# A sorted mixture-of-experts stage in a two-layer decoder: row contents, order of the start, way back of the results and home of w1

## The reference

```python
xr = x @ wg_red.T                                   # x: layer norm of the stream, 2048 x 128
wg_unit = wg / jnp.maximum(jnp.linalg.norm(wg, axis=1, keepdims=True), EPS)
logits = xr @ wg_unit.T                             # 2048 x 8
gates = jax.nn.softmax(logits, axis=1)
indices_s = jnp.argmax(gates, axis=1)
scores = jnp.max(gates, axis=1)
for e in range(E):
    mask = (indices_s == e).astype(x.dtype)[:, None]
    h = jax.nn.gelu(x @ w1[e] + b1[e], approximate=False)   # w1[e]: 128 x 512
    out = out + mask * (h @ w2[e] + b2[e])                  # w2[e]: 512 x 128
out = out * scores[:, None]
```

## Time and profile before

| | us |
|---|---|
| median of 3 runs | 1184.0 (1183.9 to 1187.14) |
| the profiled execution | 1186.93 |
| its span, first to last instruction | 1185.2 |
| busy: PE / VectorE / ScalarE / POOL | 962.1 / 793.7 / 626.2 / 355.7 |
| the last part (norm to stream addition) | from 1023 to 1178 |

### The profile page before, as it was taken

How to read it: one execution, slowest core, us unless ns; L and a number is a source line. 1 busy time by engine, 2 the same in 40 slices (tenths; PEclk the granted TensorE clock), 3 DMA queues, 4 the chain that set the end, 5 groups by cost and what they waited for, 6 DMA issues and landing times. The chain is left out here.

```text
span 1185.2 us, 20933 instructions
## 1 busy us (share of the span) xinstructions
PE 962.1 (81%) x6175; PEld 495.7 (42%) x6175; DVE 793.7 (67%) x1693; ACT 626.2 (53%) x1548; POOL 355.7 (30%) x533
## 2 busy tenths in 40 slices
PE   4489999999999736899799999999999677352870
PEld 2122233333333134566545555555555435331760
DVE  8789999999999286566556665666656689243111
ACT  4548888888888702222365656656566233110540
POOL 4212222222222131000244454545545423225004
PEclk9759999999999956799899999999999889766995
DMA  1000000000000000000100000000000100105762
GB/s 45 1 1 1 1 2 2 0 0 0 0 0 0 1 15 14 6 16 20 35 14 8 12 10 7 13 7 13 7 8 1 32 0 1 54 1 155 204 188 71
DMA packets 47723, 28.63 MB, mean 24 GB/s; under 512 B 12152, under 2 KB 44208, under 8 KB 47664
## 3 DMA queue, kind: packets, MB, share of 16 engines
q1 hardware_dynamic: 46640, 25.81, 7.9%
q0 software_dynamic: 1024, 2.10, 0.6%
HBM read 22.79 MB, written 5.11 MB: 24 GB/s over the span
## 5 line engine op out<-in xcount | busy, mean ns | idle before, releaser
L509 DVE TENSOR_REDUCE a_nmax<-a_rows 128x2 f32<-128x1024 f32 x256 | 299.2, 1218 | 14.6 <-PE a_rows L415 11.4
L552 ACT ACTIVATE a_probs<-a_turned 128x512 f32<-128x512 f32 x512 | 269.2, 603 | 40.7 <-PE a_turned L437 39.1
L1116 POOL TENSOR_TENSOR a_prob<-a_prob,a_rinv 128x256 f32<-128x256 f32 (+3 forms) x128 | 159.7, 1253 | 173.1 <-DVE a_rinv L1306 172.8
L1299 DVE TENSOR_REDUCE a_nmax<-a_score 128x2 f32<-128x256 f32 (+3 forms) x128 | 105.6, 825 | 124.2 <-PE a_score L1155 119.8
L1253 ACT ACTIVATE a_prob<-a_score,a_nmax 128x128 f32<-128x128 f32 (+3 forms) x256 | 132.7, 523 | 82.4 <-DVE a_nmax L1299 82.0
L437 PE MATMUL a_turned<-a_q,a_qk 32*128 32x512 bf16 x512 | 137.4, 391 | 7.6 <-ACT a_probs L552 5.6
L400 PE MATMUL a_acc<-a_probs,a_vg 128*32 128x512 f32 x1024 | 139.0, 615 | 0.8 <-ACT a_probs L552 0.7
L415 PE MATMUL a_rows<-a_qk 32*128 32x512 bf16 x512 | 111.9, 401 | 13.2 <-DVE a_nmax L509 6.2
L1152 PE MATMUL a_score<-a_k_s,a_q_s 64*128 64x384 f32 (+3 forms) x512 | 103.7, 481 | 2.2 <-ACT a_prob L1253 1.3
L437 PEld LDWEIGHTS a_turned<-a_q,a_qk 32*128 32x128 bf16 x512 | 35.3, 91 | 155.1 <-ACT a_probs L552 131.8
L1312 DVE COPY a_pt<-a_turn 128x128 f32<-128x128 f32 (+3 forms) x224 | 92.2, 447 | 1.4 <-PE a_turn L1166 1.4
(11 more groups left out here) (288 smaller groups left out, 1518.9 us busy)
## 6 DMA issues: line engine op xcount, KB each, us to landing
m_w<-L_ffn_w SPq DMA_DIRECT2D x46, 256.0 KB, 3.6
a_wq<-L_attn_Wq SPq DMA_DIRECT2D x16, 128.0 KB, 2.2
xs_sorted<-m_zeros SPq DMA_DIRECT2D x1, 1472.0 KB, 6.6
m_xs<-xs_sorted SPq DMA_DIRECT2D x5, 256.0 KB, 3.6
ys_sorted<-m_ysb SPq DMA_DIRECT2D x5, 256.0 KB, 3.3
g_X<-x SPq DMA_DIRECT2D x4, 256.0 KB, 3.6
m_wgu<-L_ffn_gate_up_proj SPq DMA_DIRECT2D x8, 128.0 KB, 2.1
a_wk<-L_attn_Wk SPq DMA_DIRECT2D x32, 32.0 KB, 2.0
```

What stands on the lines that cost most here:

```text
L509: dve.tensor_reduce(nmax[i % 2][:, p // 2, (p % 2) * 2:(p % 2) * 2 + 2], rows[n % 2][:, :, :], AX_X, ALU.max, negate=True).then_inc(row_ou ...
L552: act.activation(probs[:, (tb % 2) * 4 + j, :], turned[n % 3][:, :], ACT.Exp, scale=float(HD0) ** -0.5).then_inc(turn_out, 1)
L1116: pool.tensor_tensor(pr, pr, spread(rinv[:, t % RING, :], 2, width), ALU.mult).then_inc(scl, 1)
L1299: dve.tensor_reduce(nmax[:, t % RING, :], score[t % 2][:, :, 0:width], AX_X, ALU.max, negate=True).then_inc(mx, 1)
```

## The change

- The rows that are scattered carry 130 numbers instead of 128 (`ROW1`, 520 bytes): the norm, the token's number and its score. The norm is written straight into them (`xe`). Unused slots hold a number of their own beyond 2047, in `blank`.
- Results are scattered to token order by POOL in the tile loop, one indirect DMA a tile, into `y_tokens`. The address is the token number out of the sorted row. VectorE multiplies y by the score as it copies it, into a ring of four buffers, guarded by `y_out`. At the end SP loads y in token order in four DMAs, and four wide additions follow.
- The small loads go first on SP, and the blank rows follow; the statistics and the norm stand ahead of the gate weights' work on VectorE, PE, ScalarE and POOL, except for one reduction over `wg` behind `in_s`, which stands between VectorE's statistics and its normalising. The two gate matrices are folded into one of 128 x 8 (`wge`), and the logits come from XT directly.
- w1 of all experts (2 MB) is loaded once. VectorE copies the expert's 128 x 512 into one of three buffers for each tile, at an address that it loads into a register from `eid_i`. SP loads only w2 for each tile, and the up-projection waits for the copy (`s_w1`), the down-projection for w2.
- VectorE copies x of tile t after w1 of tile t, and y of tile t - 2 behind them.

Declarations and semaphore names are left out below.

```diff
 
...
             for n in range(SB * b, SB * b + SB):
-                dve.tensor_scalar(self.g.XN[:, n, :], self.g.X[:, n, :], self.mv[:, n, 0:1],
+                dve.tensor_scalar(self.rows[:, n, 0:D], self.g.X[:, n, :], self.mv[:, n, 0:1],
                                   self.rstd[:, n:n + 1], ALU.subtract, ALU.mult).then_inc(self.norm, 1)
 
     def tensor(self, pe):
...
             pe.wait_ge(self.norm, SB * (b + 1))
             wait(pe, self.xt, b - 1)
...
-        ln = LayerNorm(sc, g, ln_ps)
+        xe = sc.sb("xe", [P, NT, ROW1])
+        ln = LayerNorm(sc, g, ln_ps, rows=xe)
...
-        w1 = [sc.sb(f"w1{i}", [P, FH]) for i in range(WB)]
+        w1_all = sc.sb("w1_all", [P, E, FH])
+        w1 = [sc.sb(f"w1{i}", [P, FH]) for i in range(3)]
...
-        xs = sc.sb("xs", [P, TILES1, D])
+        xs = sc.sb("xs", [P, TILES1, ROW1])
+        token = sc.sb("token", [P, TILES1], I32)
...
-        ysb = sc.sb("ysb", [P, TILES1, D])
+        ysb = sc.sb("ysb", [P, 4, D])
...
-        xs_d = nc.dram_tensor("xs_sorted", (SLOTS1, D), F32).ap()
-        ys_d = nc.dram_tensor("ys_sorted", (SLOTS1, D), F32).ap()
+        xs_d = nc.dram_tensor("xs_sorted", (SLOTS1, ROW1), F32).ap()
+        y_d = nc.dram_tensor("y_tokens", (NT * P + SLOTS1, D), F32).ap()
...
-            sp.wait_ge(zs, 1)
-            sp.dma_start(xs_d.rearrange("(t p) d -> p t d", p=P), zeros[:, :, :]).then_inc(zd, 16)
...
+            sp.wait_ge(blank_s, 2)
+            sp.dma_start(xs_d.rearrange("(t p) d -> p t d", p=P), blank[:, :, :]).then_inc(blank_d, 16)
+            for e in range(0, E, 2):
+                sp.dma_start(w1_all[:, e:e + 2, :], g.dram["L1_ffn_w1"][e:e + 2].rearrange("e d h -> d e h")
+                             ).then_inc(w1_in, 16)
...
-                sp.dma_start(w1[t % WB][:, :], g.dram["L1_ffn_w1"][bass.ds(e, 1)].rearrange("o d h -> (o d) h")
-                             ).then_inc(w_in[t % WB], 16)
                 sp.dma_start(w2[t % WB][:, :, :],
                              g.dram["L1_ffn_w2"][bass.ds(e, 1)].rearrange("o (f p) d -> p (o f) d", p=P)
                              ).then_inc(w_in[t % WB], 16)
...
-            for t in range(T):
-                if t + WB < T:
-                    load_weights(t + WB)
-                for t0, t1 in GROUPS:
-                    if t + 1 == t1:
-                        sp.wait_ge(s_y, t1)
-                        sp.dma_start(ys_d[t0 * P:t1 * P, :].rearrange("(t p) d -> p t d", p=P), ysb[:, t0:t1, :]
-                                     ).then_inc(ys_out, 16)
+            for t in range(WB, T):
+                load_weights(t)
+
+            for i in range(4):
+                sp.wait_ge(y_out[i], 16 * len(range(i, T, 4)))
+            for b in range(B):
+                sp.dma_start(yg[:, SB * b:SB * b + SB, :],
+                             y_d[S * b:S * (b + 1), :].rearrange("(t p) d -> p t d", p=P)).then_inc(back[b], 16)
...
-            pool.memset(zeros[:, :, :], 0.0).then_inc(zs, 1)
+            pool.memset(blank[:, :, :], 0.0).then_inc(blank_s, 1)
             pool.memset(hmask[:, :], 1.0).then_inc(hm, 1)
+            pool.wait_ge(blank_s, 1)
+            pool.iota(blank[:, :, D], pattern=[[P, T]], base=NT * P, channel_multiplier=1,
+                      allow_small_or_imprecise_dtypes=True).then_inc(blank_s, 1)
...
+            pool.iota(xe[:, :, D], pattern=[[P, NT]], base=0, channel_multiplier=1,
+                      allow_small_or_imprecise_dtypes=True).then_inc(s_ext, 1)
+            ln.gpsimd(pool)
+            pool.wait_ge(wnd, 2)
+            pool.tensor_tensor(wnorm[:, 2:3], wnorm[:, 0:1], wnorm[:, 1:2], ALU.pow).then_inc(wn, 1)
...
-            pool.wait_ge(wnd, 2)
-            pool.tensor_tensor(wnorm[:, 2:3], wnorm[:, 0:1], wnorm[:, 1:2], ALU.pow).then_inc(wn, 1)
-            ln.gpsimd(pool)
-
-            pool.wait_ge(zd, 16)
+            pool.wait_ge(blank_d, 16)
+            pool.wait_ge(s_ext, 2)
             pool.wait_ge(s_pos, 1)
             for n in range(NT):
                 pool.indirect_dma_start(out=xs_d, out_offset=bass.IndirectOffsetOnAxis(ap=pos_i[:, n:n + 1], axis=0),
-                                        in_=g.XN[:, n, :], in_offset=None).then_inc(scat, 16)
-            pool.wait_ge(ys_out, 16 * len(GROUPS))
-            for n in range(NT):
-                pool.indirect_dma_start(out=yg[:, n, :], out_offset=None, in_=ys_d,
-                                        in_offset=bass.IndirectOffsetOnAxis(ap=pos_i[:, n:n + 1], axis=0)
-                                        ).then_inc(back[n // SB], 16)
+                                        in_=xe[:, n, :], in_offset=None).then_inc(scat, 16)
+            for t in range(T):
+                pool.wait_ge(s_id, t // 4 + 1)
+                pool.wait_ge(s_y, t + 1)
+                pool.indirect_dma_start(out=y_d, out_offset=bass.IndirectOffsetOnAxis(ap=token[:, t:t + 1], axis=0),
+                                        in_=ysb[:, t % 4, :], in_offset=None).then_inc(y_out[t % 4], 16)
...
+            ln.tensor(pe)
             pe.wait_ge(in_s, 16 * (3 + NT))
-            pe.transpose(flat[0][:, 0:GD], wgr[:, :], g.ident[0:GD, 0:GD]).then_inc(prep, 1)
-            pe.transpose(flat[1][:, 0:E * FC], b1r[:, :], g.ident[0:E * FC, 0:E * FC]).then_inc(prep, 1)
+            pe.transpose(up[0][:, 0, 0:E * FC], b1r[:, :], g.ident[0:E * FC, 0:E * FC]).then_inc(prep, 1)
             pe.wait_ge(wnd, 5)
-            pe.transpose(flat[2][0:GD, 0:E], wgu[:, :], g.ident[0:E, 0:E]).then_inc(prep, 1)
-            ln.tensor(pe)
+            pe.transpose(up[1][0:GD, 0, 0:E], wgu[:, :], g.ident[0:E, 0:E]).then_inc(prep, 1)
+            pe.wait_ge(prep_c, 2)
+            pe.matmul(xps[0][:, 0:E], wgr[:, :], wgut[:, :], start=True, stop=True).then_inc(prep, 1)
             pe.wait_ge(prep_c, 3)
             for b in range(B):
                 ln.ready(pe, b)
-                pe.matmul(flat[b][0:GD, :], wgrt[:, :], g.XT[:, b * S:(b + 1) * S], start=True, stop=True
-                          ).then_inc(s_xr, 1)
-            pe.wait_ge(s_xrc, B)
-            for n in range(NT):
-                last = pe.matmul(ln_ps[0][:, n * E:(n + 1) * E], xr[:, n * P:(n + 1) * P], wgut[:, :],
-                                 start=True, stop=True)
+                for n in range(SB * b, SB * b + SB):
+                    last = pe.matmul(xps[1][:, n * E:(n + 1) * E], g.XT[:, n * P:(n + 1) * P], wge[:, :],
+                                     start=True, stop=True)
...
-                pe.transpose(xps[t % 2][:, 0:P], xs[:, t, :], g.ident[:, :]).then_inc(s_xp, 1)
+                pe.transpose(xps[t % 2][:, 0:P], xs[:, t, 0:D], g.ident[:, :]).then_inc(s_xp, 1)
...
-                pe.wait_ge(w_in[t % WB], 32 * (t // WB + 1))
+                pe.wait_ge(s_w1, t + 1)
...
             def down_of(t):
+                pe.wait_ge(w_in[t % WB], 16 * (t // WB + 1))
...
-            for i, (dst, src) in enumerate(((wgrt[:, :], flat[0][:, 0:GD]), (b1t[:, :, :].rearrange("p e f -> p (e f)"), flat[1][:, 0:E * FC]),
-                                            (wgut[:, :], flat[2][0:GD, 0:E]))):
+            ln.scalar(act)
+            for i, (dst, src) in enumerate(((b1t[:, :, :].rearrange("p e f -> p (e f)"), up[0][:, 0, 0:E * FC]),
+                                            (wgut[:, :], up[1][0:GD, 0, 0:E]), (wge[:, :], xps[0][:, 0:E]))):
                 act.wait_ge(prep, i + 1)
                 act.activation(dst, src, ACT.Copy).then_inc(prep_c, 1)
-            ln.scalar(act)
-            for b in range(B):
-                act.wait_ge(s_xr, b + 1)
-                act.activation(xr[:, b * S:(b + 1) * S], flat[b][0:GD, :], ACT.Copy).then_inc(s_xrc, 1)
...
+            ln.vector_stats(dve)
             dve.wait_ge(in_s, 16 * (3 + NT))
             dve.tensor_tensor_reduce(out=wsq[:, :], in0=wg[:, :], in1=wg[:, :], scale=1.0, scalar=0.0,
                                      op0=ALU.mult, op1=ALU.add, accum_out=wnorm[:, 0:1]).then_inc(wnd, 1)
+            ln.vector_norm(dve)
...
-            ln.vector_stats(dve)
-            ln.vector_norm(dve)
-            rt.top1(dve, ln_ps[0][:, 0:NT * E].rearrange("p (n e) -> p n e", e=E))
+            rt.top1(dve, xps[1][:, 0:NT * E].rearrange("p (n e) -> p n e", e=E))
...
+            dve.wait_ge(s_ext, 1)
+            dve.tensor_copy(xe[:, :, D + 1], rt.score[:, :]).then_inc(s_ext, 1)
...
+            def copy_w1(t):
+                if t == 0:
+                    dve.wait_ge(w1_in, 16 * E // 2)
+                wait(dve, s_up, t - 2)
+                e = dve.value_load(eid_i[0:1, t:t + 1], min_val=0, max_val=E - 1)
+                dve.tensor_copy(w1[t % 3][:, :], w1_all[:, bass.ds(e, 1), :].rearrange("p o h -> p (o h)")
+                                ).then_inc(s_w1, 1)
...
             def copy_y(t):
                 dve.wait_ge(s_dn, t + 1)
-                dve.tensor_copy(ysb[:, t, :], down[t % 2][:, 0:D]).then_inc(s_y, 1)
-
-            copy_x(0)
+                if t >= 4:
```

(44 more changed lines are left out.)

16 lines of the change are left out of this document (9 added, 7 removed).

## The result

The changed kernel takes 1145.7 us (median of 4, 1144.86 to 1147.15) against 1183.95, a ratio of 0.9686 with a 95% interval of 0.9642 to 0.9729. Its profiled execution took 1146.02 us with a span of 1144.3; the one of before took 1186.93. So 40.9 us went between the two profiles, where 41.8 was forecast.

The account below looks back on a forecast made before the run. One chain bounds the last stage: loads behind zeros, a loop bound by weight traffic, then gathers. -15.0 + 0.6 - 11.9 - 15.5 = -41.8 takes 1186.9 to 1145.1 us profiled, 1142.2 median; range 1137 to 1159.

Parts of the forecast that it names:

- Head: Last stage's start up to the logits: small loads first and norm ahead of gate work save 15.0 us (bounds -10.9, -16.3).
- the term of the logits: End of the head: 32 logit passes, now with 128-row weights, keep about 5.5 us.
- Routing and scatter: Between logits and tile loop: w1 copies beside scatters add 0.4 us, a cast 0.2; +0.6 (bounds 0, +5).
- The cover of the score's copy: Routing: copying the score into the rows hides in VectorE's wait for the rank matmuls, costing nothing; uncovered 0.2 us.
- Rival B: Scatter and sorted-row load: 520-byte rows may move as two pieces, doubling landing and first load; +5 us, 1147; chance 0.08.
- Loop: Tile loop: without w1 on the DMA queue, 19 steps take 1.92 us each; -11.9 us (bounds -13.5, -10).
- VectorE's 1.9 us in line: Tile loop: y copy 0.29, register load 0.73, w1 copy 0.39, x copy 0.28 and gaps, one after another per tile.
- rival E: Tile loop: w2 alone still arrives late, landing over 5.5 us after issue, so no loop gain; 1154 us; chance 0.03.
- the sum for w2: Tile loop: w2's register load to issue 0.73, 0.38, landing at most 4.3; 5.4 us against some 6.6 available.
- Rival A: Tile loop: VectorE bounds it, each w1 copy waiting for a scatter (0.96); adds 9 or 18 us, 1151 to 1160; chance 0.19.
- the rule: Tile loop: VectorE's two-port copies lock out GpSimd's DMA descriptor writes, so w1's copies would delay POOL's scatters.
- Tail: After the last y copy: one scatter, four loads and one addition take 9.8 us against 25.3; -15.5 (bounds -16.5, -12.4).

Follow-up runs that it names:

- h1: Changed kernel, but SP waits for the blank rows and writes them before the small loads, as before; 1153.65 us, head 28.70 against 22.07.
- u1: Changed kernel, but w1 is loaded by DMA for each tile again, without the VectorE copies; 1153.58 us, loop 53.88 against 43.61.
- u2: Changed kernel, but y is stored in sorted order and gathered by POOL at the end again; 1160.86 us, tail 24.31 against 9.69.
- l2: Changed kernel with the register load on VectorE done twice for each tile; 1148.18 us, loop 47.07 against 43.61.
- n1: Changed kernel with the 16 b2 loads on their own semaphore, so the normalising no longer waits for them; 1148.74 us, head 19.84 against 22.07.
- l1: Changed kernel with w1 copied twice for each tile, register load once; 1146.27 us, loop 44.70 against 43.61.
- l4: Changed kernel with w1 copied four times for each tile; 1154.71 us, loop 51.99 against 43.61.
- l3: Changed kernel meant to copy w1 four times; by a slip one extra copy, behind a wait standing three times; 1150.11 us, loop 45.51 against 43.61.

## Why the prediction was right, point by point

*What bounded the kernel.* All three stretches were named rightly, and undoing each change alone gives its time back: 6.6 us of the head with h1 (8.0 at equal logits), 10.3 of the loop with u1, 14.6 of the tail with u2. The rest of the head's gain, from the norm ahead of the gate weights and from the folded gates, was not undone by itself; it is read from the two timelines.

*Head, -15.0 forecast, -13.1 measured.* The small loads took 6.8 us (6.4), the first work behind them came at 7.9 us of the stage (7.6), the last tile was normalised at 12.2 (12.1), and the logits began at 15.0 (14.6). Up to there the sum was 0.4 us short. The other 1.5 is the term of the logits: 5.5 forecast, 7.00 measured. It is the one step of the head that failed. I backed it with the weight loads of the norm's transposes, 0.18 us each, and had no bound above it; the eight passes of the loop's first up-projection at the low clock take 2.05 us, 0.26 each, which gives 8.2. But the taller weights are not what was missed. The 5.51 us of before were not all at the low clock, as I had read them. In stretches, first before (the norm's transposes up to 1049.5, the reduction to 1053.7, then the logits), then after:

```profile
1047.00:1048.40 1.40, 1.40 (x7) 0.87 (x5) 1.15 (x5) 0.77 (x2) 0.63 (x1) 0.50 0.00 0
1048.60:1049.50 0.90, 0.67 (x5) 0.50 (x6) 0.18 (x1) 0.60 (x1) 0.00 (x0) 1.00 0.00 0
1049.50:1053.70 4.20, 3.53 (x8) 0.61 (x8) 0.00 (x0) 2.94 (x5) 0.00 (x0) 1.00 0.01 4
1053.70:1055.30 1.60, 1.60 (x15) 1.60 (x15) 0.00 (x0) 0.00 (x0) 0.00 (x0) 1.00 0.00 0
1055.50:1059.20 3.70, 3.70 (x18) 3.62 (x17) 0.00 (x0) 0.00 (x0) 0.00 (x0) 0.50 0.00 0
```

```profile
1038.40:1045.50 7.10, 7.00 (x32) 6.90 (x32) 0.01 (x1) 0.00 (x0) 0.00 (x0) 0.50 1.02 308
```

In before 15 passes took 1.60 us at 1.00, 0.11 each, and the rest 0.21 each at 0.50. After, all 32 ran at 0.50, 0.22 each. So a pass with 128 rows of weights costs what one with 16 rows does, and the whole 1.5 us is the clock's. Why it was up in before is not shown. It had risen during the transposes and stayed up through the reduction that the change removes; but h1 and l2 began the logits at 1.00 without a reduction, and nine other profiles at 0.50.

*Routing and scatter, +0.6 forecast, +0.2 measured.* The cover of the score's copy held. One scatter took 1.15 us instead of 0.96 beside the w1 copies (in n1 none did), and not two by 0.2. Rival B (520-byte rows) did not come: the last scatter landed after 2.30 us (at least 2.2 before) and the first rows after 2.83, where 2.82 is before's.

*Loop, -11.9 forecast, -11.7 measured.* The step is 1.90, PE's. The forecast took VectorE's 1.9 us in line. That step was too dear: from the register load's start (1122.35) to the w1 copy (1123.08) are 0.73 us, just SP's, but the y copy runs beside it, so only 0.40 shows. With that VectorE needs 1.90 - 0.53 = 1.37 us a tile, and 0.5 are to spare; l1 shows that a second copy of 0.43 nearly fits. That VectorE's forecast work came out at PE's 1.90 was chance, and did no harm because PE's own 1.90 was right. The w1 copy took 427 ns, where L1515 had 394. The first three steps, kept at 6.95, took 7.42 (1080.42 to 1087.84), and the other 19 took 36.19, where the forecast had 36.5 (19 x 1.92).

*w2 and rival E.* The 2.7/3.4/4.3 that the earlier trace rows call w2's landing are those of w1's loads (L1680). The row of w2's own, in before from 1090 to 1153:

```profile
L1682 SPq DMA_DIRECT2D m_w<-L_ffn_w x19: 373/380/1372, 1100.2 to 1145.1; - x19
...
DMA to landing us min/median/max: 3.0/4.1/4.7
```

With 4.7 in place of 4.3 the sum for w2 is 5.8 us instead of 5.4, still inside the 6.6 that it has, so the misread row changed nothing. PE never waited for w2.

*Rival A and the rule.* The loop is not held up: scatters and copies that overlap (l4, l3, l1) lengthen each other by at most 0.2 us, and PE bounds the step. The Trainium skill, page "SBUF — State Buffer", section "SBUF: two separate sides", states that descriptors of POOL's DMAs wait for a two-port copy of VectorE. The traces don't agree on a wait of that length. With copies queued from 1120.23 to 1121.76 in l4, the scatter of 1120.57 takes its 0.96 us, and no first packet of a scatter starts later than 1.73 us behind POOL's row, where 1.53 is the least. Whether the 0.2 us that do show are such a wait, no run here tells. Beside the tensor_tensor of 2048 numbers a partition the fourth scatter again took 1.96, as in the earlier trace rows; by which means no run here tells.

*Tail, -15.5 forecast, -15.6 measured.* The scatter was taken up later (1.12 against 0.7), landed a little sooner (2.3 against 2.4), and the loads took 5.5 (5.8).

*From the profile to the median.* The forecast took off 2.9 us, by which the profiled execution of before lay above its median; that of the changed kernel lies only 0.3 above. That accounts for 2.6 of the 3.5 us between 1142.2 and 1145.7, and the sum's own 0.9 (1145.1 against 1146.02) for the rest.

## What to carry to other kernels

Where a stage is one chain, cut it at the landmarks of the timeline, cost each piece from its own rows, and compare pieces, not whole times, when the other stages vary by more than the effect. Before a price is taken from the "nearest" row, check that it is the same operation at the same granted clock, and split a row wherever the clock changes inside it: a mean over both levels is a price at neither. An overlap that a rule forbids is best tested by making more of it and reading each row's length, not the median alone. Small loads that gate work belong ahead of a large transfer on their queue, and on a semaphore of their own.
